# A selective-scan kernel in which GpSimd makes the product of units 2, 5 and 7 of each tile, in place of every third unit

## The reference

```python
def step(h, inp):
    u_t, d_t, b_t, c_t = inp
    dA = jnp.exp(d_t[..., None] * A[None])
    h = dA * h + (d_t * u_t)[..., None] * b_t[:, :, None, :]
    y = jnp.einsum('bkdn,bkn->bkd', h, c_t)
    return (h, y)
```

## Time and profile before

| | |
|---|---|
| median of 3 runs | 37435.4 us (37430.31 to 37442.24) |
| profiled execution | 37436.43 us |
| its span, first to last instruction | 37434.6 us |
| mean granted TensorE clock | 0.814 of full |
| busy: PE, DVE, ACT, POOL | 73%, 90%, 51%, 83% |
| instructions on PE, DVE, ACT, POOL | 77616, 18423, 23286, 7776 |

### The profile page before, as it was taken

The page is one execution under the profiler, slowest core; times in us unless marked ns, Lnnn a source line. Parts: engine busy times, 40 slices in busy tenths (PEclk is TensorE's granted clock), DMA queues, the critical chain, the costliest instruction groups (busy, mean ns, idle before and its releaser), DMA issues. The chain is left out here.

```text
span 37434.6 us, 335995 instructions
## 1 busy us (share of the span) xinstructions
PE 27489.6 (73%) x77616; PEld 7503.9 (20%) x77616; DVE 33867.2 (90%) x18423; ACT 19017.1 (51%) x23286; POOL 31107.2 (83%) x7776
## 2 busy tenths in 40 slices
PE   5777777777766777777777766777777777766777
PEld 2111111111122111111111112111111111112114
DVE  6999999999977999999999977999999999976993
ACT  4555555555534555555555534555555555534551
POOL 1999999999962999999999962999999999974994
PEclk7888888888878888888888878888888888877886
DMA  4666666666675666666666675666666666675665
GB/s 152 165 165 168 165 164 166 164 163 165 165 232 174 165 164 165 163 165 164 165 163 163 164 227 174 165 164 163 166 164 166 163 165 165 164 230 184 165 163 176
DMA packets 2388306, 6376.98 MB, mean 170 GB/s; under 512 B 691536, under 2 KB 836304, under 8 KB 2376400
## 3 DMA queue, kind: packets, MB, share of 16 engines
q1 hardware_dynamic: 2386640, 6362.76, 63.4%
HBM read 2961.86 MB, written 764.47 MB: 100 GB/s over the span
## 5 line engine op out<-in xcount | busy, mean ns | idle before, releaser
L1262 POOL TENSOR_TENSOR h<-h,c 128x2048 f32<-128x2048 f32 x4992 | 20800.0, 4176 | 2260.4 <-DVE h L1062 1988.6
L1062 DVE TENSOR_TENSOR_SCAN h<-decay,state,slot 128x1024 f32<-128x1024 f32 x6656 | 15625.1, 2348 | 814.5 <-ACT state L1206 33.2
L968 PE MATMUL psy<-h,t_fold 128*32 128x512 f32 x40000 | 11515.0, 746 | 0.0
L898 PE MATMUL slot<-bc,pick 96*128 96x512 bf16 x13328 | 4969.0, 466 | 7855.6 <-DVE h L1058 4802.3
L1036 DVE TENSOR_TENSOR slot<-du,slot 128x1024 f32<-128x1024 f32 x6656 | 8048.1, 1209 | 675.1 <-PE slot L898 569.1
L1101 ACT ACTIVATE decay<-delta,na 128x1024 f32<-128x1024 f32 x6664 | 7570.4, 1145 | 1817.4 <-DVE h L1062 1640.1
L1283 POOL TENSOR_TENSOR made<-du,b 128x2048 f32<-128x2048 f32 x1664 | 7531.6, 4526 | 151.3 <-DMA b<-bcdram 121.9
L1058 DVE TENSOR_TENSOR_SCAN h<-slot,state,made 128x1024 f32<-128x1024 f32 x3328 | 7609.3, 2327 | 4.6 <-ACT slot L1101 4.5
L1101 ACT ACTIVATE slot<-delta,na 128x1024 f32<-128x1024 f32 x3328 | 3716.7, 1117 | 6373.7 <-DVE h L1062 6367.5
L968 PEld LDWEIGHTS psy<-h,t_fold 128*32 128x32 f32 x40000 | 2165.1, 127 | 7917.9 <-issue 7576.5
L898 PEld LDWEIGHTS slot<-bc,pick 96*128 96x128 bf16 x13328 | 868.5, 104 | 13935.0 <-DVE h L1058 7655.2
(11 more groups left out here) (111 smaller groups left out, 18699.7 us busy)
## 6 DMA issues: line engine op xcount, KB each, us to landing
delta<-delta SPq DMA_DIRECT2D x10048, 128.0 KB, 2.6
du<-du SPq DMA_DIRECT2D x10048, 128.0 KB, 2.7
c<-bcdram SPq DMA_DIRECT2D x6720, 128.0 KB, 2.8
b<-bcdram SPq DMA_DIRECT2D x6688, 128.0 KB, 3.0
u<-useq SPq DMA_DIRECT2D x212, 1536.0 KB, 6.6
yseq<-ybuf SPq DMA_DIRECT2D x624, 512.0 KB, 2.9
ya<-yseq SPq DMA_DIRECT2D x420, 512.0 KB, 4.3
yb<-yseq SPq DMA_DIRECT2D x360, 512.0 KB, 5.3
```

Of the source, the lines that this page charges most:

```text
L898: mm = pe.matmul(slot[s % 2][:, cols], pick[:, rows_of, :], bc[q % 2][:, cols], start=True, stop=True)
L968: mm = pe.matmul(psy[rows, cols], T["fold"][:, :], h[v % H_RING][:, c, cols], start=(v % QUADS == 0), stop=(v % QUADS == QUADS - 1), skip_ ...
L1062: dve.tensor_tensor_scan(out, decay[s % DECAY_RING][:, order], slot[s % 2][:, order], first, ALU.mult, ALU.add).then_inc(sem["h_ready"], 1)
L1262: pool.tensor_tensor(both[:, :, 0:CH], both[:, :, 1:], c4[g][:, order].unsqueeze(1).broadcast_to((P, 2, CH)), ALU.mult)\
```

## The change

```diff
-POOL_EVERY, POOL_LEAD = 3, 2
+POOL_UNITS, POOL_LEAD = (2, 5, 7), 2
@@ scan_stage
-    on_pool = [v for v in range(BU) if v % POOL_EVERY == POOL_EVERY - 1]
+    on_pool = [v for v in range(BU) if v % TILE_UNITS in POOL_UNITS]
```

## The result

The changed kernel takes 36577.21 us (median of 4 runs, 36574.1 to 36582.95), the kernel before, beside it, 37438.7 (37430.31 to 37442.24). The ratio is 0.977, with a 95% interval of 0.9753 to 0.9787: faster, by 861.5 us. The forecast was 36585, 8 us too high. The profiled execution took 36579.95 us, with a span of 36576.4.

What follows compares the result with a forecast made beforehand. VectorE was taken to bound the kernel, held up by TensorE in a few places. 37436.4 - 562 (exchange) - 320 (waits for fills) + 30 (ScalarE's decay) = 36584, say 36585 us; range 36490 to 36900.

Steps and rivals of the forecast that it cites:

- The exchange: On VectorE, one unit a chunk goes from 7.18 to 4.48 us as GpSimd makes its product: 562 us saved.
- The waits for fills: VectorE's waits for TensorE's fill of slot before its products in the scan stages all go: 320 us, bounds 0 to 319.7.
- The four places: Unit 2 of the second and third tile in both chunks of a body, where VectorE waits for TensorE's fill.
- Rival 1: The stalls stay, TensorE being late for unit 3 or more at 1.2 GHz: 36875 us, chance 0.12 wholly or in part.
- ScalarE's decay: VectorE's waits for ScalarE's decay at unit 2 could come in six tiles a body, not two: 30 us added.
- GpSimd keeps up: GpSimd's tile costs 48.9 us against VectorE's 49.34, 0.45 us of slack, so its added product stays hidden.
- The layout of a tile: Units laid end to end: GpSimd waits for VectorE's unit 1, and its product for unit 7 has 2.3 us to spare.
- The wait for b: GpSimd waits about 1.5 us once a chunk, in the third tile, for b behind c transfers; cost on the path 0.
- another 1 us: The further delay of b in the third tile at which GpSimd's hidden wait would start to show.
- rival 2: GpSimd becomes the bound, with a wait for b of 1.4 us in every tile: 36968 us, chance 0.05.
- rival 3: Slower: SyncE's queue delays b for unit 2 by 3.2 us in all tiles: 38090 us, chance 0.04 together with rival 4.
- Rival 4: GpSimd and VectorE exclude each other, each added product holding VectorE 4.53 us: 37875 us, chance 0.04 together with rival 3.

Runs made afterwards that it cites:

- place alone: Changed kernel with eight products a chunk as before, GpSimd taking units 2 and 5 of the first tile and 2, 5, 7 of the others: 37150.21 us, ratio 0.992.
- unit 1 and 4 kernel: Changed kernel, still nine products a chunk, with GpSimd's units 1, 4 and 7 in place of 2, 5 and 7 in second and third tiles: 36626.45 us, ratio 0.978.

## Why the prediction was right, step by step

- **The exchange, 562 us.** Right. Nine products placed alike against eight placed alike gave 573 in the runs and 559 in the stages of the traces. The two unit lengths of the earlier trace rows were enough: what the 559 consist of is 505 of busy time and 45 of short gaps before scans, and little else.
- **The waits for fills, 320 us.** Right in place and size. The four places lost all 319.7 us, place alone gave 298 in the runs, and taking work off TensorE in the kernel before gave 327. Rival 1 (they stay or move on to unit 3) is out: the waits inside the stages are 28.8 us, and none stands before unit 3. The argument for it, though, was only half the cause. The prediction named the work ahead of the fill and put the clock beside it ("partly at 1.2 GHz"). The unit 1 and 4 kernel, where I expected the waits back, shows that the work ahead isn't enough: with TensorE at 2.4 GHz there, they don't come.
- **ScalarE's decay, 30 us.** Right in sign, too large: the waits for it before GpSimd's units rose by 8 us (4.5 to 12.3), all idle time there by 10. Two small waits that no step named came with the change: 27.7 us before the second product of unit 6, and 15.5 before the first scan of unit 1 in 32 first tiles. The total is within 8 us of the measured one because errors of this size went both ways; that much of it is luck.
- **GpSimd keeps up.** Right: VectorE waited for its products 1.7 us, in 6 times. But the step had it wait for VectorE before the gate of unit 1 of every tile, and that is wrong. All its waits for VectorE before a gate are 93.6 us in the whole execution, where they were 2260.3. The layout of a tile had no waits for b. They make GpSimd late for a chunk's first tile, and it works that off over the tiles: counted over the trace, the gate of unit 1 of the first, second and third tile starts 1.7, 0.9 and 0.3 us after its scans in the first chunk of a body, and 2.2, 1.5 and 0.9 us after in the second (medians). Work of 146.7 us by the pitches and waits for b of 480/208 = 2.3 make 149.0 us a chunk; VectorE's chunk is 298.0/2 = 149.0. The two engines are tied.
- **The wait for b, 1.5 us once a chunk, hidden.** Hidden: yes, since taking all of it away moved nothing (36576 against 36577). It stands where the prediction put it, at the end of a third tile, but it is 2.3 us and not 1.5. That it stays hidden is in part luck. By the prediction's own numbers a wait of 1.5 us a chunk is more than three tiles at 0.45 can work off (1.35). It was covered because VectorE's chunk, with its own waits, took 149.0 us and not 148.0, which leaves GpSimd 2.3 us a chunk. Nor was there a reserve of "another 1 us": one gate later for b raised the waits by 2.3 us a chunk (2.3 to 4.6) and cost 491/208 = 2.4. One case, with 1.71 us: GpSimd's timeline over the end of a chunk, and SyncE's queue over the same stretch.

```profile
5107.98 4.54 POOL L1283 TENSOR_TENSOR made<-du,b 128x2048 f32<-128x2048 f32 x1
5112.47 12.41 POOL L1262 TENSOR_TENSOR h<-h,c 128x2048 f32<-128x2048 f32 x3
5126.59 4.51 POOL L1283 TENSOR_TENSOR made<-du,b 128x2048 f32<-128x2048 f32 x1 [1.71 <-DMA b<-bcdram]
```

```profile
5108.06 1.70 SPq L762 DMA_DIRECT2D c<-bcdram  x4
5109.80 4.96 SPq L777 DMA_DIRECT2D du<-du  x8
5114.80 5.05 SPq L777 DMA_DIRECT2D delta<-delta  x8
5119.96 1.91 SPq L762 DMA_DIRECT2D c<-bcdram  x4
5121.91 1.81 SPq L762 DMA_DIRECT2D b<-bcdram  x4
```

  The queue is the one the prediction wrote down: c, du, delta, c, b without a gap, b's issue over at 5123.72 and b there 2.87 us later.
- **Rival 2 and 3** were the near misses. One gate's delay of b turns rival 2 on (37069, where the forecast priced it at 36968), and ten products a chunk make a loss of 1.8% against the kernel before, where rival 3 had priced one (38136 against 38090): by a tenth product of 4.49 us a chunk and 3.0 us more of waits for b in the same queue. The forecast's chances for them, 0.05 and part of 0.04, stood on a slack that the waits for b used up.
- **Rival 4** is out for this kernel by the products' unchanged 1208 ns, and shown as a mechanism by the kernel with two inputs in SBUF. (The busy times that the prediction added up against it make 64974.4 us, not 64974.8; nothing hangs on it.)

No kernel here beats the changed one by more than the runs can tell: 36576 and 36572 us with b loaded earlier.

## What to carry to other kernels

When two engines share a list of units, price a unit by its pitch on each, starts to starts, and balance the chunk with the waits for loads counted in: here the first 2.3 us of them a chunk cost nothing and the next 2.3 cost 2.4. Give the helper those units before which a third engine is late: here the place of eight products was worth 298 us and the ninth product 573. Before such a trade, see where the operands of the pair lie: with one in PSUM the engines run side by side, with both in SBUF this kernel loses 23%.

## What the runs showed of the chip that I had not expected

- TensorE can be busy without a gap and still be granted 1.2 GHz: 9.00 of 9.00 us busy at 0.51 in the window above, while the same projection and fold in another chunk took 3.9 us in place of 7.4 at 1.00. Whether VectorE waited for the fill behind them in the kernel before went with that (130 third tiles to 78, without an exception).
- GpSimd and VectorE take turns by whole instructions when a scan has both tensors in SBUF (a gate of 6.13 us, 4.17 and one scan): 2327 to 4543 ns for the scan, 4182 to 4912 for the gate, 36577 to 44852 us for the kernel.
- A late load reaches VectorE by a way that its own waits don't name: with b one gate later, more of its lost time was put down to TensorE's fills (231 us) than to GpSimd's products (217).
